# Three constant matmuls ahead of the wait for an item's sums, in a deformable convolution

## The chip, the cores and the metric

The kernel runs on one core of a Trainium2 chip. Five engines with a queue of instructions each work side by side and meet at semaphores: PE (matrix multiplications and transposes, results to PSUM), DVE and ACT (arithmetic on tiles), POOL (here it issues the gathers and does some additions), SP (plain DMAs). The metric is the device time of one execution, in microseconds (us). Lower is better.

## What is computed

The input x is f32 of shape (4, 128, 48, 48). Two stages with residual additions:

```
x = x + deformable_conv(group_norm(x))     # 3x3, then batch norm over all images, ReLU
x = x + conv3x3(group_norm(x)) + bias
```

The deformable convolution first computes 27 maps with an ordinary 3x3 convolution: for each of the nine taps a shift in y, a shift in x and a mask (a sigmoid). Each output point then reads, for each tap, four neighbouring points of the normalised image around the shifted position, weights them bilinearly, multiplies by the mask, and a 128x128 matrix per tap turns the 128 channels into outputs, summed over the taps.

## The kernel before, in words

The image points are cut into 24 chunks (ALL) of 384 points, six per image. A chunk has three tiles of 128 points and nine taps, so 27 pairs of tap and tile. Pairs are worked on in items of three: in most chunks an item is one tap over the three tiles; in the first and the last chunk (BY_TILE) an item is three taps of one tile, and the very last item is cut in two. There are 217 items in all, numbered s in the code.

One item passes through these steps:

- POOL issues one indirect DMA per pair (L377), which gathers for 128 points the four neighbours with 128 channels each from a table in HBM into g. It runs ahead of the rest: before item s it waits until the transposes of item s - 4 are done (semaphore turned, LEAD = 4).
- ACT weighs the first neighbour (L644, into a PSUM bank PA), DVE the three others (L858), and DVE adds the four up in three additions (L870, L872, L874). The last one writes acc and raises sum_step.
- PE transposes the item's three tiles (turn_item, L484) from acc into one of two PSUM banks, TP[s % 2], columns 0 to 383 of 512, and raises turned.
- ACT copies the bank to cols (copy_cols, L625) and raises copied. In most chunks ACT does so for the item two before the one that it has just weighed (copy_lag).
- PE multiplies cols by the tap's matrix into the chunk's bank CO (conv_item, L472), waiting for copied. This too runs two items behind the transposes, or one in tile-wise chunks (conv_lag).

PE's own order within an item is written out in its loop: a part of the offset convolution for a chunk two ahead (offset_conv, L432, one or two taps in most items), then the conv of an earlier item with its wait for copied, then turn_item with its wait for sum_step. At some items more follows: transposes of offsets (L441) and of masks (L447), and sums for the next image's group norm. DVE computes positions, weights and indices of the next chunk in between (indices, L797 to L833), starting from PE's transposed offsets.

The kernel already has matmuls whose results nobody reads: warm_up (L427) multiplies gavg, a constant 128x128 matrix, by itself into a bank that is free. It runs at the start, around the batch norm, and with three matmuls in items 4, 5 and 6 of the last chunk. f32 matmuls are recorded as two MATMULs and two weight loads each, f32 transposes as one of each.

After the last item come the batch norm's statistics, the ReLU, the second group norm and the second convolution, which are not touched.

Of the kernel before, what the change touches and what calls it, by code (L numbers as in the profile page):

```python
# [9 lines left out]
P = 128  # L10
# [5 lines left out]
CP = TILES * P  # L16
# [69 lines left out]
def items(c):  # L86

    if c not in BY_TILE:
        return [[(k, t) for t in range(TILES)] for k in range(TAPS)]
    return [[(k, t) for k in taps] for t in range(TILES) for taps in (LAST_SETS if (c, t) == (ALL - 1, TILES - 1) else TAP_SETS)]  # L90


def first_item(c):
    return sum(len(items(i)) for i in range(c))
# [15 lines left out]
def part_count(c):  # L110

    return c + 2
# [25 lines left out]


WARM_ITEMS = (4, 5, 6)  # L140
BANDS = 4
BR = H // BANDS
BP = BR * W
# [11 lines left out]
def build(nc, x_d, tab_d, woff_d, wconv_d, w1_d, boff_d, par_d, grid_d, out_d):  # L155

    with ExitStack() as ctx:
        def sb(name, shape, dt=F32):
            return ctx.enter_context(nc.sbuf_tensor(name, shape, dt))

        def ps(name):
            return ctx.enter_context(nc.psum_tensor(name, [P, 512], F32))

        def sem(name):
            return ctx.enter_context(nc.semaphore(name))
# [21 lines left out]
        gavg = sb("gavg", [P, P])  # L187
# [17 lines left out]
        wt0 = sb("wt0", [P, 2, TILES, 9])  # L205
        bst = sb("bst", [P, 2 * BANDS, 6])
        mv = sb("mv", [P, 2])
# [17 lines left out]
        TP = (ps("TP0"), ps("TP1"))  # L225
# [37 lines left out]
        sum_step = sem("sum_step")  # L263
# [45 lines left out]
        def add_band(eng, b, j):  # L309
            s = b * HW + j * BP  # L310
            return eng.tensor_tensor(x[:, s:s + BP], x[:, s:s + BP], o[:, s:s + BP], ALU.add)  # L311
# [10 lines left out]
        def _(sp):  # L322
# [11 lines left out]
            sp.dma_start(w1[:], w1_d).then_inc(w1_in, 16)  # L334
            for n in range(B * BANDS):
                sp.wait_ge(finished, 2 * n + 2)
                sp.dma_start(out_d[:, n * BP:(n + 1) * BP], x[:, n * BP:(n + 1) * BP]).then_inc(stored, 16)
            sp.wait_ge(stored, 16 * B * BANDS)

        @block.gpsimd  # L340
        def _(pl):
# [40 lines left out]
            def add(b):  # L382
                for j in range(0, BANDS, 2):
                    pl.wait_ge(relued, b * BANDS + (BAND_ORDER.index(j) + 1))
                    add_band(pl, b, j).then_inc(added, 1)
# [20 lines left out]
        def _(pe):  # L406
# [70 lines left out]
            def turn_item(c, i):  # L477
                units = items(c)[i]
                s = first_item(c) + i
                pe.wait_ge(sum_step, (s + 1) * 4)  # L480
                if c in BY_TILE and s > 1:
                    pe.wait_ge(copied, s - 1)
                for n in range(len(units)):
                    last = nc.tensor.transpose(TP[s % 2][:, n * P:(n + 1) * P], acc[:, s % SUMS, n, :], ident[:])  # L484
                last.then_inc(turned, 1)
# [24 lines left out]
            for c in range(ALL):  # L510
# [3 lines left out]
                for k in range(len(items(c))):  # L514
# [8 lines left out]
                    while convs <= first_item(c) + k - conv_lag(c) and (c, k) != (ALL - 1, len(items(c)) - 1):  # L523
                        conv_item(*order[convs])
                        convs += 1
                    if c == ALL - 1 and k in WARM_ITEMS:
                        pe.wait_ge(wt_ready, part_count(c))
                        warm_up(3, OMT)
                    turn_item(c, k)
                    if ahead and turn_place(c + 1) == (c, k):  # L530
                        turn_offsets(part_count(c + 1) - 1)
# [497 lines left out]
```

## Time and profile before

| | |
|---|---|
| Time of the runs | 1061.64, 1062.0 and 1064.07 us, median 1062.0 us |
| Profiled execution | span 1061.3 us from first to last instruction; no other time of it is recorded |
| PE | 763.8 us (72%), 2436 MATMULs |
| DVE, ACT | 803.4 us (76%), 378.9 us (36%) |
| POOL | 669.4 us (63%) |
| Mean granted TensorE clock | 0.780 of full speed |
| Indirect gathers | 648, 169.91 MB |

Busy times are shares of the span. The granted clock has two levels here, 0.5 (1.2 GHz) and 1.0 (2.4 GHz); a mean in between is a mixture of them. In rows of the timeline the columns are start, duration, engine, line, operation, tiles out and in, count, and in brackets the idle time of the engine before it with what ended it. "remote" stands there where the semaphore changed at a time that no recorded end of an instruction explains, "issue" where the profile shows nothing that was waited for.

### The profile page before, as it was taken

To read this page: it belongs to the slowest core of one execution; us is meant where nothing else is said; L and a number is where in the kernel's file an instruction comes from. 1 tells how busy PE (TensorE), PEld (TensorE's weight loads), DVE (VectorE), ACT (ScalarE), POOL (GpSimd) and SP (SyncE) were. 2 spreads that over 40 slices of the span, in tenths; PEclk is the share of its full clock that TensorE was granted. 3 is DMA by queue.
4 is the path that set the end of the run, shared out by engine and by line. 5 is a ranking of instruction groups with operands and counts; after the bars stand their busy time and mean duration, and the time that the engine had idled before them with its cause. 6 is when DMAs were issued, how large, how long until landed. Compare 5 with 4: busy or idle time off the path is not lost.

```text
span 1061.3 us, 8955 instructions
## 1 busy us (share of the span) xinstructions
PE 763.8 (72%) x2436; PEld 354.9 (33%) x2436; DVE 803.4 (76%) x1533; ACT 378.9 (36%) x1026; POOL 669.4 (63%) x731
## 2 busy tenths in 40 slices
PE   6787777676766867666768667674776676579998
PEld 5342222322222222222223223221222222267776
DVE  3788788787878778786878778786888787867664
ACT  2333334433333335333424334332433333343320
POOL 3666666666666666666666666666666667635661
PEclk9677677778768668977867867976878775579999
DMA  8666666666666666666566665666666666630111
GB/s 290 185 171 185 187 191 185 176 189 184 185 178 188 186 183 189 189 189 182 166 185 191 189 187 169 186 186 181 181 186 189 186 188 189 175 113 23 51 50 56
DMA packets 56245, 181.38 MB, mean 171 GB/s; under 512 B 11012, under 2 KB 12036, under 8 KB 55812
## 3 DMA queue, kind: packets, MB, share of 16 engines
q0 software_dynamic: 51840, 169.91, 55.8%
q1 hardware_dynamic: 3924, 10.32, 2.6%
q10 hardware_dynamic: 432, 0.59, 0.2%
q8 instruction: 19, 0.31, 0.1%
q14 instruction: 30, 0.25, 0.1%
HBM read 176.06 MB, written 4.72 MB: 170 GB/s over the span
## 4 chain that ended last, share of the span: by engine, by line
POOL 39%; issue 16%; DVE 16%; PE 14%; another core or an unknown queue 10%; DMA 3%; ACT 2%; DVEq 0%; POOLq 0%; ACTq 0%
POOL g L377 39%; DVE g L858 5%; DMA g<-corner_table,idx 3%; DVE PA L870 2%; DVE PA L872 2%; PE TP L564 2%; PE PA L564 2%; PE CO L564 2%; DVE acc L874 2%; PE OMT L432 2%; PE TP L484 1%; PE VU L564 1%; PE OMT L564 1%; PE CO L472 1%
## 5 line engine op out<-in xcount | busy, mean ns | idle before, releaser
L377 POOL DMA_INDIRECT g<-corner_table,idx x648 | 613.5, 947 | 327.5 <-issue 188.9
L472 PE MATMUL CO<-cols,wcs 128*128 128x384 f32 (+1 forms) x504 | 261.2, 622 | 123.2 <-issue 64.7
L644 ACT ACTIVATE PA<-g,wt 128x128 f32<-128x128 f32 x642 | 203.0, 357 | 400.2 <-DMA g<-corner_table,idx 171.5
L858 DVE TENSOR_TENSOR g<-g,PA 128x1152 f32<-128x1152 f32 (+1 forms) x217 | 291.3, 1342 | 68.6 <-DMA g<-corner_table,idx 58.9
L432 PE MATMUL OMT<-xn,woff 128*27 128x384 f32 (+2 forms) x450 | 208.4, 576 | 43.1 <-DVE wt L828 21.7
L484 PE MATMUL TP<-ident,acc 128*128 128x128 f32 x648 | 145.1, 344 | 118.5 <-DVE acc L874 60.3
L472 PEld LDWEIGHTS CO<-cols,wcs 128*128 128x128 f32 x504 | 94.1, 241 | 285.8 <-issue 186.0
L484 PEld LDWEIGHTS TP<-ident,acc 128*128 128x128 f32 x648 | 92.4, 173 | 261.0 <-DVE acc L874 114.5
L870 DVE TENSOR_TENSOR PA<-g,PA 128x384 f32<-128x384 f32 x214 | 120.3, 562 | 59.6 <-ACT PA L644 22.9
L872 DVE TENSOR_TENSOR PA<-g,PA 128x384 f32<-128x384 f32 x214 | 120.3, 562 | 18.1 <-DVE PA L870 7.6
L874 DVE TENSOR_TENSOR acc<-g,PA 128x384 f32<-128x384 f32 x214 | 118.4, 553 | 15.2 <-DVE PA L872 4.9
L625 ACT ACTIVATE cols<-TP 128x384 f32<-128x384 f32 (+1 forms) x217 | 102.0, 470 | 66.9 <-remote 46.1
L432 PEld LDWEIGHTS OMT<-xn,woff 128*27 128x27 f32 x450 | 39.2, 115 | 109.8 <-issue 78.7
L319 POOL TENSOR_TENSOR g<-xn 128x288 f32<-128x288 f32 (+1 forms) x60 | 41.5, 726 | 31.7 <-ACT xn L719 30.5
L458 PE MATMUL CO<-vt,ut 9*128 9x384 f32 (+1 forms) x56 | 35.6, 730 | 0.0
L797 DVE SCALAR_TENSOR_TENSOR low<-OMT,grid 128x54 f32<-128x54 f32 (+2 forms) x25 | 5.2, 208 | 34.5 <-remote 27.0
L607 ACT ACTIVATE mask<-OMT 128x27 f32<-128x27 f32 (+2 forms) x25 | 4.8, 192 | 62.4 <-remote 23.9
L618 ACT ACTIVATE vt<-VU 9x384 f32<-9x384 f32 x24 | 11.4, 476 | 43.2 <-remote 31.0
L427 PE MATMUL PA<-gavg 128*128 128x128 f32 x128 | 18.2, 306 | 2.9 <-POOL gavg L354 2.6
L447 PE MATMUL VU<-ident,vsum 128*9 128x128 f32 x72 | 16.0, 346 | 4.2 <-issue 4.2
L611 ACT ACTIVATE std<-OMT,eps 128x1 f32<-128x1 f32 x4 | 1.0, 262 | 50.4 <-PE OMT L413 50.4
L311 POOL TENSOR_TENSOR x<-x,o 128x576 f32<-128x576 f32 x8 | 12.1, 1524 | 10.9 <-ACT o L707 10.8
(132 smaller groups left out, 545.8 us busy)
## 6 DMA issues: line engine op xcount, KB each, us to landing
g<-corner_table,idx POOLq DMA_INDIRECT x648, 3.4
out_dram<-x SPq DMA_DIRECT2D x16, 288.0 KB, 2.1
x<-x_dram SPq DMA_DIRECT2D x3, 1152.0 KB, 7.6
x<-x_dram ACTq DMA_DIRECT2D x3, 192.0 KB, 4.0
x<-x_dram SPq DMA_DIRECT2D x3, 192.0 KB, 3.8
wconv<-wconv_dram SPq DMA_DIRECT2D x1, 576.0 KB, 5.0
w<-w_dram SPq DMA_DIRECT2D x1, 576.0 KB
grid<-grid_dram SPq DMA_DIRECT2D x1, 162.0 KB, 4.1
```

Source lines behind the costliest of these rows:

```text
L319: return eng.tensor_tensor(mixed[:, m, first:first + rows, :], p, q, op)
L377: pl.indirect_dma_start(out=g[:, k, t].rearrange("p q c -> p (q c)"), out_offset=None, in_=tab_d, in_offset=bass.IndirectOffsetOnAxis(ap=i ...
L432: last = nc.tensor.matmul(OM[:, first * W:(first + rows) * W], woff[:, k, :], xn[:, row + k // 3:row + k // 3 + rows, k % 3:k % 3 + W], st ...
L472: last = nc.tensor.matmul(co_bank(c, t)[:, t * P:t * P + size], wcs[:, c // CHUNKS % 2, k, :], cols[:, s % TURNS, n * P:n * P + size], sta ...
L484: last = nc.tensor.transpose(TP[s % 2][:, n * P:(n + 1) * P], acc[:, s % SUMS, n, :], ident[:])
L564: last = nc.tensor.matmul(MX[h % 2][m][:, 0:HB], w, mixed[:, m, r:r + BR, :], start=(ky == 0), stop=(ky == 2))
L625: nc.scalar.activation(cols[:, s % TURNS, 0:size], TP[s % 2][:, 0:size], ACT.Copy).then_inc(copied, 1)
L644: last = nc.scalar.activation(first[:, n] if s < LAST_SUMS else g[:, k, t, 0, :], g[:, k, t, 0, :], ACT.Copy, scale=wt0[:, c % 2, t, k:k + 1])
L858: nc.vector.tensor_tensor(corners[:, :, 1:4, :], corners[:, :, 1:4, :], weights[:, :, 1:4].unsqueeze(3).to_broadcast([P, size, 3, P]), ALU ...
L870: nc.vector.tensor_tensor(some, corners[:, :, 1, :], some, ALU.add).then_inc(sum_step, 1)
L872: nc.vector.tensor_tensor(some, corners[:, :, 2, :], some, ALU.add).then_inc(sum_step, 1)
L874: nc.vector.tensor_tensor(acc[:, s % SUMS, 0:size, :], corners[:, :, 3, :], some, ALU.add).then_inc(sum_step, 1)
```

## The change

PE's turn_item issues three matmuls of gavg by gavg into columns 384 to 511 of the bank that the item's transposes will fill. They stand ahead of the wait for the item's sums. The wait for copied, which tile-wise chunks have, comes before them, since it guards the bank.

```
+KEEP_WARM = 3
...
             def turn_item(c, i):
                 units = items(c)[i]
                 s = first_item(c) + i
-                pe.wait_ge(sum_step, (s + 1) * 4)
                 if c in BY_TILE and s > 1:
                     pe.wait_ge(copied, s - 1)
+                for _ in range(KEEP_WARM):
+                    nc.tensor.matmul(TP[s % 2][:, CP:CP + P], gavg[:], gavg[:], start=True, stop=True)
+                pe.wait_ge(sum_step, (s + 1) * 4)
                 for n in range(len(units)):
                     last = nc.tensor.transpose(TP[s % 2][:, n * P:(n + 1) * P], acc[:, s % SUMS, n, :], ident[:])
                 last.then_inc(turned, 1)
```

Nothing else is changed.

## Rows read from the trace of the kernel before

**Rows 1.** The page's shares of the chain that ended last, by engine.
```profile
POOL 39%; issue 16%; DVE 16%; PE 14%; another core or an unknown queue 10%; DMA 3%; ACT 2%; DVEq 0%; POOLq 0%; ACTq 0%
```

**Rows 2.** Windows: stretch, length, each engine's busy time, granted clock, DMA share, GB/s.
```profile
16.20:944.40 928.20, 641.52 (x1848) 256.17 (x1847) 724.48 (x1337) 343.82 (x971) 613.51 (x648) 0.75 0.64 185
...
589.50:593.00 3.50, 0.17 (x1) 0.00 (x0) 3.03 (x5) 0.88 (x4) 0.60 (x2) 0.79 0.52 146
593.00:598.30 5.30, 5.28 (x12) 2.08 (x12) 2.91 (x5) 1.69 (x5) 4.08 (x5) 0.50 0.52 147
598.40:608.00 9.60, 6.34 (x22) 2.37 (x21) 7.15 (x9) 3.81 (x12) 7.16 (x9) 1.00 0.73 209
885.00:919.00 34.00, 19.93 (x43) 8.76 (x43) 27.56 (x52) 11.99 (x35) 22.73 (x24) 0.50 0.63 183
```

**Rows 3.** Groups: count, busy us, mean ns, idle before and what ended it.
```profile
L377 POOL DMA_INDIRECT g<-corner_table,idx x648 | 613.5, 947 | 327.5 <-issue 188.9
...
L484 PE MATMUL TP<-ident,acc 128*128 128x128 f32 x648 | 145.1, 344 | 118.5 <-DVE acc L874 60.3
```

**Rows 4.** Timeline of POOL's gathers, three of them after a long wait.
```profile
571.32 0.94 POOL L377 DMA_INDIRECT g<-corner_table,idx  x1 [2.55 <-remote]
...
592.71 0.94 POOL L377 DMA_INDIRECT g<-corner_table,idx  x1 [2.90 <-remote]
593.96 0.94 POOL L377 DMA_INDIRECT g<-corner_table,idx  x1 [0.30 <-issue]
...
600.21 0.95 POOL L377 DMA_INDIRECT g<-corner_table,idx  x1 [0.31 <-issue]
...
738.42 0.94 POOL L377 DMA_INDIRECT g<-corner_table,idx  x1 [3.94 <-remote]
```

**Rows 5.** POOL's waits: total us, times, longest.
```profile
POOL g L377 <- remote: 99.1, 34, 3.9
...
POOL g L377 <- PE TP L484: 23.7, 12, 3.5
```

**Rows 6.** Timeline of PE around the gather at 592.71.
```profile
588.25 0.55 PE L484 MATMUL TP<-ident,acc 128*128 128x128 f32 x3 [0.94 <-DVE acc L874]
...
593.02 1.65 PE L472 MATMUL CO<-cols,wcs 128*128 128x384 f32 x2 [3.34 <-ACT cols L625]
594.46 0.85 PE L484 MATMUL TP<-ident,acc 128*128 128x128 f32 x3
```

**Rows 7.** Timeline of ACT in the same stretch.
```profile
592.47 0.49 ACT L625 ACTIVATE cols<-TP 128x384 f32<-128x384 f32 x1 [2.62 <-remote]
```

**Rows 8.** Timeline of PE over the last items.
```profile
940.84 1.49 PE L427 MATMUL OMT<-gavg 128*128 128x128 f32 x6
942.12 0.85 PE L484 MATMUL TP<-ident,acc 128*128 128x128 f32 x3
...
944.50 0.83 PE L427 MATMUL OMT<-gavg 128*128 128x128 f32 x6
945.16 0.49 PE L484 MATMUL TP<-ident,acc 128*128 128x128 f32 x3
...
948.08 0.94 PE L472 MATMUL CO<-cols,wcs 128*128 128x128 f32 x6 [0.58 <-ACT cols L625]
948.96 0.44 PE L484 MATMUL TP<-ident,acc 128*128 128x128 f32 x2
950.31 0.33 PE L484 MATMUL TP<-ident,acc 128*128 128x128 f32 x1 [0.91 <-DVE acc L868]
```

**Rows 9.** Timeline of PE and POOL at the first transposes.
```profile
31.16 0.81 PE L484 MATMUL TP<-ident,acc 128*128 128x128 f32 x3
...
33.49 0.94 POOL L377 DMA_INDIRECT g<-corner_table,idx  x1 [2.44 <-PE TP L484]
```

**Rows 10.** Timeline of DVE at the last item's sums.
```profile
949.96 0.29 DVE L868 TENSOR_TENSOR acc<-g 128x128 f32<-128x128 f32 x1
```

**Rows 11.** Timeline of ACT and DVE in the last chunk.
```profile
931.59 0.49 ACT L625 ACTIVATE cols<-TP 128x384 f32<-128x384 f32 x1 [5.71 <-remote]
...
934.56 0.56 DVE L870 TENSOR_TENSOR PA<-g,PA 128x384 f32<-128x384 f32 x1 [5.00 <-ACT PA L644]
```

More of the change, by code:

```diff
@@ L140 @@
 WARM_ITEMS = (4, 5, 6)
+KEEP_WARM = 3
 BANDS = 4
@@ L479, in turn_item @@
                 s = first_item(c) + i
-                pe.wait_ge(sum_step, (s + 1) * 4)
                 if c in BY_TILE and s > 1:
                     pe.wait_ge(copied, s - 1)
+                for _ in range(KEEP_WARM):
+                    nc.tensor.matmul(TP[s % 2][:, CP:CP + P], gavg[:], gavg[:], start=True, stop=True)
+                pe.wait_ge(sum_step, (s + 1) * 4)
                 for n in range(len(units)):
```

## The prediction

> **What bounds it now.** I read the page first. The chain that ended last is POOL's for 39%, and 10% stands under "another core or an unknown queue" [rows 1]. PE is no bound by that view: it is busy 641.5 us of the 928.2 us from the first gather to the last [rows 2], a stretch I call the gather stage. Next the groups by line: POOL issues 648 gathers of 947 ns [rows 3], one each 1.25 us, because 0.30 or 0.31 us of issue time follows each [rows 4]. That makes 648 x 1.25 = 810 us, so 118 us of the stage go elsewhere. POOL's waits name them: 34 waits on "remote" with 99.1 us and 12 on PE's transposes with 23.7 us [rows 5].
>
> The timeline shows what such a wait is. PE's transposes that start at 588.25 are over at 588.80, and every earlier item's too [rows 6]. ACT's copy of a turned item still starts only at 592.47, after 2.62 us on "remote" [rows 7], and POOL's next gather at 592.71 [rows 4]. So both see PE's count of turned items late, some 2.6 us after POOL has stopped issuing. The length of these waits is regular. After 12 gathers without one it is 2.55 us, after 15 2.90, after 21 3.94 [rows 4], the gathers between counted in the same view. Each gather issued adds (3.94 - 2.55) / 9 = 0.15 us to the next wait, whatever PE, ACT and DVE did in between. 648 x 0.15 = 97 us, most of the 118. I read this as a debt that POOL's pace runs up and pays at the next stop: an earlier or later stop changes when it is paid, hardly how much. Why the count is seen late no row shows.
>
> **What the change adds.** Each of the 217 items gets three f32 matmuls of 128x128 on gavg, recorded as two MATMULs each, so 1302 MATMULs and as many weight loads. They wait for nothing new: the wait on copied, which stands in tile-wise chunks alone, only moves ahead of the wait on sums and was met before the conv in front of it. They signal nobody. No DMA is added, and nothing on ACT, DVE or POOL.
>
> Their price stands in the trace, because the last chunk already runs three such matmuls ahead of three of its items. At half clock the six MATMULs start at 940.84 and the transposes behind them at 942.12: 1.28 us. At full clock, 944.50 to 945.16: 0.66 us [rows 8]. Over 217 items that is 143 to 278 us of PE time; at the stage's mean granted clock of 0.75 [rows 2], half of the time at each level, 210 us.
>
> What covers it: PE idles 118.5 us in front of its transposes, waiting for sums [rows 3]. That is exactly where the new matmuls stand, so at most 118 us lie beside DVE's work. The rest, 92 us or 0.4 us an item, with 1.28 at most in any one, pushes transposes later. PE's idle time in front of a conv is no cover: it stands there before it reaches the new matmuls.
>
> What a later transpose costs: the gather of an item asks for the transposes of four items before. Those at 594.46 to 595.31 [rows 6] are what the gather at 600.21 needs, and it waits for nothing beyond its 0.31 us [rows 4]: 4.9 us of slack in an item just after a late count, where PE is furthest behind. If PE comes out of such a stop at half clock, as here, it does one or two items with 1.28 us more each, 2.6 us, and keeps 2.3 us. Where the slack is gone, POOL stops a little earlier and, by the debt above, waits less at the next stop. I take 0 for the gather stage. Bounds: below, 10 us off, from the chain view of the stage (the first rival); above, 15 us on (the second). Between them stand the 12 waits on transposes, 23.7 us in all, the only ones where PE's own lateness is on record.
>
> What the matmuls may give: a fuller PE and a higher clock. From 885 to 919 PE has 19.93 us of work in 34 and the granted clock is 0.50 throughout [rows 2]; with 1.28 us more for each of some eight items it is busy some 30 of 34. Three transposes take 0.85 us at half clock and 0.49 at full [rows 8]. That makes PE quicker between its waits, but PE is not what its neighbours wait for; I count it as paying for the 92 us, no more.
>
> A rule speaks against the gain, and the trace bears it out first: from 589.5 to 593 PE does 0.17 us of work, and from 593 to 598.3 it has 0.50, in full use [rows 2]. The Trainium skill (TensorE: Matmul & The Clock Gate, section "Why this matters for your kernels") says that idle gaps between bursts of matmuls bring the lower clock back. The stops that make these gaps stand before a conv, with the added matmuls behind it, so by the rule the clock falls there as before and the sum stays at no gain.
>
> The head: the first transposes start at 31.16, and POOL's fifth item waits for them until 33.49 [rows 9]. PE has no idle time there, so they come 1.28 us later at half clock; POOL loses between 0 (if the count would have been seen late anyway) and 1.3 us. I take 0.6.
>
> The tail: DVE hands over the last sums at 949.96 + 0.29 = 950.25 [rows 10] and the last transpose follows at 950.31 [rows 8], so PE is on time by 0.06 us. The items turned at 945.16 and 948.96, with one between, follow each other through transposes, ACT's copy and a conv, 1.9 us a round, and each round gets 0.66 us more; PE shows no idle time in front of 948.96 that would hide it. Three rounds of 0.66 and the 0.66 of the last item itself, less the idle 0.91 us in front of 950.31 [rows 8], make +1.7. Against it, a higher clock ahead of 943 brings PE into these rounds earlier: by 0.36 us for the transposes and 0.7 for the conv (1.65 at half clock [rows 6], 0.94 at full [rows 8]), so 1.1 us if one item is affected and 2.2 if two have piled up. I take the first, +0.6, with ends at -0.5 and +1.7.
>
> Sum: 1061.3 (the span) + 0 + 0.6 + 0.6 = 1062.5 us. The median of the runs is 1062.0, 0.7 above the span, so on their scale 1063.2.
>
> One thing spreads this without a sign. In the last chunk one late count holds ACT for 5.71 us and through it DVE for 5.00 [rows 11]. Where the stops fall shifts with every microsecond, and a chunk of 38 us has one or two of them. I allow 4 us either way.
>
> **Rivals.** First, faster: the clock stays full and the pieces of the chain where PE itself is late at half clock shrink. For it: the 0.50 of a 34 us stretch, and 12 POOL waits with PE as releaser. The Trainium skill (same page, section "Part 4: PE-mode transpose") says that transposes don't raise the clock as matmuls do; these added ones are matmuls. Against it: the debt, which would be paid anyway. Price: half of the 23.7 us off and the 1.2 of head and tail on, -10.6: 1051 us. Chance 0.17.
>
> Second, slower: PE oversubscribed at half clock. An item then needs one offset tap, a conv (1.65), transposes (0.85) [rows 6, 8] and 1.28 more; with the tap taken as long as the conv, 5.4 us, over the stage's 928.2 / 217 = 4.28. If the clock doesn't rise while PE catches up, three or four items in a row fall behind by 1.1 us each and eat the 4.9 us of slack. From there on POOL stops on transposes. It decides where the slack is under 2 us; if the 12 waits on transposes become twice as many with the same 2 us, less what later stops give back, it is about +15: 1078 us. Against it: from 598.4 on the clock is at full after such a stop already now [rows 2]. Chance 0.15.
>
> Third, slower by more: the delay with which PE's count is seen grows with the number of PE's instructions, which rises by 0.7 in the stage (1302 on 1848 MATMULs [rows 2]). For it: only PE's signals are late. Against it: the length of the waits follows the gathers alone. Price, if the 99.1 us grow by half as much as the instructions, 0.35: +35, 1097 us. Chance 0.06.
>
> That the matmuls don't lift the clock at all, so that the change doesn't do what it is for, leaves the forecast where it is; it is inside its 0.62.
>
> **Numbers.** The forecast holds 0.62, with 1058 to 1069 as its own range. With 4 us of scatter around +1.2 it gives same (within 0.3%, 3.2 us, which is what a measurement of this kernel can tell) 0.40, slower 0.15, faster 0.07. With the rivals: faster 0.24, same 0.40, slower 0.36. The range of 1053 to 1080 leaves out half of the first rival, the third and the far part of the second, some 0.18.
>
> **What would show it.** Right: POOL's "remote" waits again near 99 us in 30 to 40 pieces, 0.15 us per gather, PE busier by about 200 us and its idle time before the transposes nearly gone, the mean clock of the stage above 0.75 and the time unchanged. The first rival shows as POOL waits on PE's transposes well under 23.7 us and a gather stage shorter by ten; the second as those waits doubled; the third as "remote" waits that are longer for the same number of gathers. I am wrong at the root if the waits on "remote" change their slope, because then PE does take part in the debt.

## The result and the profile after

The changed kernel takes 1075.4 us, the kernel before 1063.0 us beside it on the same chip (medians of four runs each). The ratio is 1.0114, 95% interval 1.0094 to 1.0133: 12.4 us slower. The range of 1053 to 1080 holds that, but the likeliest case does not, whose own range ended at 1069. The profiled execution of after took 1077.5 us with a span of 1075.7, 14.4 above the span of before.

PE first, where the added work is. From the page of after the line of PE, then the chain by engine.

```profile
PE 826.4 (77%) x3738; PEld 523.6 (49%) x3738; DVE 805.7 (75%) x1533; ACT 378.5 (35%) x1026; POOL 670.3 (62%) x731
...
POOL 29%; PE 28%; issue 16%; another core or an unknown queue 10%; DVE 10%; DMA 4%; ACT 3%; SPq 0%; DVEq 0%; ACTq 0%; POOLq 0%
```

The groups by line of after (count, busy us, mean ns, idle before), and its gather stage as a window (the columns of [rows 2]):

```profile
L378 POOL DMA_INDIRECT g<-corner_table,idx x648 | 614.4, 948 | 337.9 <-issue 177.6 <-remote 111.0 <-PE TP L487 34.5
L484 PE MATMUL TP<-gavg 128*128 128x128 f32 x1302 | 210.4, 305 | 2.6 <-issue 2.6
L487 PE MATMUL TP<-ident,acc 128*128 128x128 f32 x648 | 124.9, 307 | 23.4 <-issue 11.3 <-DVE acc L877 8.6 <-DVE PA L875 2.5
```

```profile
16.00:955.60 939.60, 700.37 (x3123) 420.84 (x3122) 727.27 (x1337) 343.38 (x971) 614.35 (x648) 0.87 0.63 184
```

The added matmuls are busy on PE for 210.4 us. The 210 of the prediction counted something else, from the start of the added matmuls to the start of the transposes; summed that way over the trace of after, idle time left out, it is 187 us. PE's idle time before the transposes fell from 118.5 us [rows 3] to 23.4, the granted clock of the stage rose from 0.75 [rows 2] to 0.87, and the transposes went from 344 to 307 ns. Yet PE's share of the chain doubled from 14% [rows 1], and the stage grew from 928.2 us to 939.6. That is +11.4 of the 14.4; the other 3 lie after the last gather (9.5 us to the last transposes there, 6.3 before).

POOL's gathers cost the same. What grew is the idle time in front of them, 327.5 us [rows 3] to 337.9, and POOL's waits in after (total us, times, longest) say in which way:

```profile
POOL g L378 <- remote: 111.0, 47, 3.1
POOL g L378 <- PE TP L487: 34.5, 18, 3.2
```

There were 34 and 12 of them before [rows 5], so 46 became 65: more waits, not longer ones. The timeline of POOL in after shows the new pattern; the lines left out between two of these are 11 gathers with 0.30 or 0.31 us in front.

```profile
827.67 0.94 POOL L378 DMA_INDIRECT g<-corner_table,idx  x1 [2.58 <-remote]
...
844.95 0.95 POOL L378 DMA_INDIRECT g<-corner_table,idx  x1 [2.55 <-remote]
...
862.21 0.95 POOL L378 DMA_INDIRECT g<-corner_table,idx  x1 [2.54 <-PE TP L487]
```

The same stretch before; 17 gathers without a stop are left out between the first two lines, 14 between each of the next:

```profile
807.88 0.94 POOL L377 DMA_INDIRECT g<-corner_table,idx  x1 [3.00 <-remote]
...
833.55 0.94 POOL L377 DMA_INDIRECT g<-corner_table,idx  x1 [3.46 <-remote]
...
854.92 0.94 POOL L377 DMA_INDIRECT g<-corner_table,idx  x1 [2.91 <-remote]
...
876.36 0.94 POOL L377 DMA_INDIRECT g<-corner_table,idx  x1 [2.97 <-remote]
```

A stop after 12 gathers waits 2.55 us in after, just as before [rows 4]. The medians over all stops (defined below) say the same: 2.56, 2.98 and 3.44 us after 12, 15 and 18 gathers before; 2.09, 2.58 and 2.97 us after 9, 12 and 15 in after. The slope is untouched. But starts lie 17.28 us apart over 12 gathers and 25.67 over 18, so a gather costs 8.39 / 6 = 1.398 us, and 17.28 - 12 x 1.398 = 0.50 us is left over that is paid by the stop. I call a gap of over 0.7 us in front of a gather a stop. Counted so, the profile of before has 46 and that of after 62: 16 more at 0.50 are 8 of the 10.4 us of added idle time. The remaining 2.4 I can't put in one place. The line does not hold for the shortest distances: stops after only three gathers, four in each profile, wait 1.6 to 2.9 us, where it gives 1.2.

### The profile page after: what moved, and what is told of

The parts are those of the page before. It is cut to its first block, busy times and chain, and to the rows that moved or that the text cites. A ratio compares the mean times of both kernels' runs of the same rounds, so it can differ in the third digit from the quotient of the medians.

```text
span 1075.7 us, 11542 instructions
## 1 busy us (share of the span) xinstructions
PE 826.4 (77%) x3738; PEld 523.6 (49%) x3738; DVE 805.7 (75%) x1533; ACT 378.5 (35%) x1026; POOL 670.3 (62%) x731
## 4 chain that ended last, share of the span: by engine, by line
POOL 29%; PE 28%; issue 16%; another core or an unknown queue 10%; DVE 10%; DMA 4%; ACT 3%; SPq 0%; DVEq 0%; ACTq 0%; POOLq 0%
POOL g L378 29%; PE CO L473 5%; PE TP L484 4%; PE OMT L433 4%; DMA g<-corner_table,idx 4%; PE TP L487 3%; DVE g L861 3%; PE TP L567 2%; PE PA L567 2%; PE CO L567 2%; DVE PA L873 1%; DVE PA L875 1%; ACT PA L647 1%; DVE acc L877 1%
## 5 line engine op out<-in xcount | busy, mean ns | idle before, releaser
L378 POOL DMA_INDIRECT g<-corner_table,idx x648 | 614.4, 948 | 337.9 <-issue 177.6
L473 PE MATMUL CO<-cols,wcs 128*128 128x384 f32 (+1 forms) x504 | 227.7, 550 | 164.2 <-issue 102.1
L484 PEld LDWEIGHTS TP<-gavg 128*128 128x128 f32 x1302 | 209.0, 221 | 69.3 <-issue 28.3
L473 PEld LDWEIGHTS CO<-cols,wcs 128*128 128x128 f32 x504 | 82.9, 214 | 297.9 <-issue 209.9
L433 PE MATMUL OMT<-xn,woff 128*27 128x384 f32 (+2 forms) x450 | 181.4, 510 | 47.6 <-DVE wt L831 25.4
L484 PE MATMUL TP<-gavg 128*128 128x128 f32 x1302 | 210.4, 305 | 2.6 <-issue 2.6
L487 PE MATMUL TP<-ident,acc 128*128 128x128 f32 x648 | 124.9, 307 | 23.4 <-issue 11.3
L487 PEld LDWEIGHTS TP<-ident,acc 128*128 128x128 f32 x648 | 86.4, 159 | 37.4 <-issue 21.1
L433 PEld LDWEIGHTS OMT<-xn,woff 128*27 128x27 f32 x450 | 36.5, 107 | 103.0 <-issue 72.5
L459 PE MATMUL CO<-vt,ut 9*128 9x384 f32 (+1 forms) x56 | 25.3, 535 | 0.0
```

What stands on the lines that cost most here:

```text
L378: pl.indirect_dma_start(out=g[:, k, t].rearrange("p q c -> p (q c)"), out_offset=None, in_=tab_d, in_offset=bass.IndirectOffsetOnAxis(ap=i ...
L433: last = nc.tensor.matmul(OM[:, first * W:(first + rows) * W], woff[:, k, :], xn[:, row + k // 3:row + k // 3 + rows, k % 3:k % 3 + W], st ...
L473: last = nc.tensor.matmul(co_bank(c, t)[:, t * P:t * P + size], wcs[:, c // CHUNKS % 2, k, :], cols[:, s % TURNS, n * P:n * P + size], sta ...
L484: nc.tensor.matmul(TP[s % 2][:, CP:CP + P], gavg[:], gavg[:], start=True, stop=True)
```

## Why are there more stops? Theories

Both POOL's gather at 844.95 and ACT's copy below wait for the transposes of item 187, which end at 837.18 + 0.55 = 837.73 in after:

```profile
837.18 0.55 PE L487 MATMUL TP<-ident,acc 128*128 128x128 f32 x3
...
840.91 0.55 PE L487 MATMUL TP<-ident,acc 128*128 128x128 f32 x3 [0.27 <-DVE acc L877]
...
845.26 0.91 PE L473 MATMUL CO<-cols,wcs 128*128 128x384 f32 x2 [3.04 <-issue]
846.01 1.30 PE L484 MATMUL TP<-gavg 128*128 128x128 f32 x6
847.10 0.85 PE L487 MATMUL TP<-ident,acc 128*128 128x128 f32 x3
```

```profile
844.71 0.49 ACT L628 ACTIVATE cols<-TP 128x384 f32<-128x384 f32 x1 [2.28 <-remote]
```

So PE's release (the raising of the semaphore that others wait for) comes 7.0 us late at two receivers at the same moment, in the last quarter microsecond of POOL's stop, as in [rows 4, 6, 7]. PE itself is not held up meanwhile: it goes on to the next item and has turned that too by 841.46, so late instructions for PE don't explain it. Of the 24 copies by ACT in the trace of before that start over 1 us after their transposes, with ACT idle for over 0.5 us in front, 21 start inside a stop of POOL; in after 36 of 38. POOL waits for the same release, so this alone doesn't show which of the two ends the other. That the length of a stop follows the gathers before it, and e5 below, speak for POOL's stop letting the release through.

- **Theory A:** after a stop PE's releases arrive at once until a certain number of PE instructions has started. Later ones are held until POOL stops again. More PE instructions per item bring the stops closer together, and each has a fixed price.
- **Rival B:** PE's added time makes its own transposes late.
- **Rival C:** fuller columns or the higher clock disturb the others.

## Experiments

All ratios are against the kernel before, run beside each kernel on the same chip, with 95% intervals. The kernel before took 1063 to 1072 us on these chips, so the microseconds in the expectations are to be read against its 1062.

**The same count with one column, and a third of the count with the same columns.**

```
-  matmul(TP[s % 2][:, CP:CP + P], gavg[:], gavg[:], ...)          # three times
+  matmul(TP[s % 2][:, CP:CP + 1], gavg[:], gavg[:, 0:1], ...)     # e1: three times
+  matmul(TP[s % 2][:, 0:CP], gavg[:], wconv[:, 0:3, :], ...)      # e2: once
```

> As the changed kernel, but each of the three added matmuls moves 1 column in place of 128: the same number of PE instructions, little PE time. Theory A (a release by PE reaches POOL late once some number of PE instructions has followed it, so POOL stops more often, about 66 times in place of 44, and each stop has a fixed price of about 0.45 us): slower than before by 8 to 14 us, about 1072 to 1077, POOL's waits on remote events near 111 us as in the changed kernel. Rival B (the added PE time makes the transposes and convolutions late): as before, 1060 to 1065, remote waits near 99 us. Rival C (the higher granted clock, or what PE's busier columns do to the rest): as before as well, as nearly no columns are added.

> As the changed kernel, but one matmul of 384 columns an item in place of three of 128: the same columns and PE time added, a third of the PE instructions. Theory A (count of PE instructions): a third of the changed kernel's loss, 1065 to 1068, some 50 stops of POOL. Rivals B and C (PE time, clock): as the changed kernel, 1073 to 1078.

Measured: e1 1.0168 (1.0142 to 1.0195), e2 1.0038 (1.0019 to 1.0057). The groups of the added matmuls, e1 and then e2:

```profile
L484 PE MATMUL TP<-gavg 128*128 128x1 f32 x1302 | 204.0, 272 | 0.0
```

```profile
L484 PE MATMUL TP<-wconv,gavg 128*128 128x384 f32 x434 | 210.8, 573 | 0.0
```

e2 adds the same PE time as the change, 210.8 against 210.4 us, and costs a third of its loss: rival B falls. (Counted from start to start, as in the prediction, it is 187 us in both.) e1 adds nearly no columns, its granted clock over the run stays at 0.771 (before 0.780, after 0.889), and it loses more, not nothing: rival C falls. e1's expectation was wrong on one thing, since a one-column matmul still takes 272 ns: its PE time isn't little, so e1 alone does not speak against B. Theory A's 1.003 to 1.006 for e2 is hit; for e1 it gave up to 14 us, 1.013, too little.

The count itself can be read from windows that start where a release got through, 0.25 us before POOL's gather, and end at the end of two successive transposes, the last that arrived in time and the first that was held. The numbers in brackets are PE's matmuls and weight loads. Before, then after, e1 and e2:

```profile
786.20:796.39 10.19, 9.65 (x27) 4.04 (x28) 7.57 (x12) 3.75 (x11) 7.57 (x8) 0.67 0.59 166
786.20:800.16 13.96, 11.87 (x33) 4.71 (x33) 10.57 (x15) 5.05 (x14) 10.40 (x11) 0.76 0.64 178
```

```profile
827.40:834.10 6.70, 6.12 (x26) 3.84 (x27) 3.21 (x5) 2.39 (x7) 4.91 (x6) 0.75 0.51 152
827.40:837.72 10.32, 9.74 (x43) 5.68 (x44) 6.60 (x10) 4.00 (x12) 7.61 (x9) 0.83 0.57 166
```

```profile
855.85:862.96 7.11, 6.55 (x23) 5.01 (x24) 3.62 (x5) 2.78 (x8) 5.34 (x6) 0.50 0.50 152
855.85:868.24 12.39, 11.84 (x39) 8.28 (x40) 8.49 (x25) 5.10 (x15) 9.40 (x10) 0.50 0.62 176
```

```profile
827.75:838.13 10.38, 8.29 (x31) 3.90 (x32) 6.66 (x10) 4.13 (x12) 7.69 (x9) 1.00 0.58 171
827.75:841.75 14.00, 11.74 (x42) 5.24 (x43) 9.50 (x13) 5.30 (x15) 10.44 (x11) 1.00 0.61 179
```

In these windows the last good release comes 6.7 to 10.4 us after the stop, the first held one 10.3 to 14.0. In instructions that is 47 to 63 and 66 to 87. The table has the medians over every stop that comes at least three items after the one before it. "Held" are the transposes that the stopped gather asks for, "in time" those of one item earlier; times and counts run to their ends. The last column is PE's busy time up to the held ones.

| kernel | stops counted | in time: us, PE instructions | held: us, PE instructions | PE busy, us |
|---|---|---|---|---|
| before | 39 | 11.0, 55 | 15.5, 71 | 12.1 |
| after | 54 | 6.5, 51 | 10.3, 78 | 8.4 |
| e1, one column | 56 | 6.0, 48.5 | 10.3, 77.5 | 8.8 |
| e2, one wide matmul | 46 | 9.8, 52 | 13.9, 73 | 11.4 |
| e11, fewer taps (below) | 35 | 14.5, 53 | 18.5, 66 | 14.0 |

From kernel to kernel the times change by a factor of 2.4 (in time) and 1.8 (held), PE's busy time by 1.7, the counts by less than 1.2. The middle between the two counts is 60 to 65 in all five. That is theory A's footprint. It holds for medians: for single stops the middle half of the held counts runs from 66 to 75 before and from 72 to 90 in after. The number of stops goes with it: 46 before, 52 in e2, 62 in after, 66 in e1. The losses over the added stops are 0.7 us a stop in e2, 0.8 in after and 0.9 in e1, more than the 0.50 of the line, so a part of a stop's price stays unexplained.

**POOL one item further ahead.** `LEAD = 4` becomes 5 in the changed kernel (e3) and in the kernel before (e4); the five buffers of sums allow it.

> The changed kernel with POOL allowed to run 5 items ahead of the transposes in place of 4. Theory A: the stops come up to 5 items apart in place of 4, some 52 in place of 66, so about 0.45 us x 14 = 6 us faster than the changed kernel, 1067 to 1070. Rivals B and C: POOL's lead hides lateness of 1 us more, or changes nothing: 1073 to 1078 by C, between 1064 and 1070 by B.

> The kernel before with POOL allowed to run 5 items ahead in place of 4. Theory A: the stops, 5 to 6 items apart now, come 6 to 7 items apart, some 36 in place of 44, so 3 to 4 us faster than before: 1058 to 1060. If the lead doesn't set the stops (the wait on remote events is a debt by the gather, whenever it is paid): no change, 1061 to 1064.

Measured: 1.0179 (1.0153 to 1.0204) and 1.0097 (1.0074 to 1.0120), both slower than with a lead of 4. My arithmetic that the lead spaces the stops was wrong: e4 has 56 stops against 46, 12 of them after three gathers, and e3 has 70. The median distance stays at 15 gathers in e4 and falls from 12 to 9 in e3, so a longer lead spaces nothing. Theory A foresaw both the wrong way; why the short stops appear is open.

**POOL off PE's releases.** POOL waits for DVE's sums, and DVE waits for the transposes that free a buffer of sums.

```
-  pl.wait_ge(turned, first_item(c) + i - LEAD + 1)
+  pl.wait_ge(sum_step, (first_item(c) + i - LEAD + 1) * 4)
   ...
+  if s >= SUMS:
+      dve.wait_ge(turned, s - SUMS + 1)          # ahead of the write to acc
```

> The kernel before, but POOL waits for the sums of the item four back (a release by DVE) in place of its transposes (a release by PE), and DVE itself waits for the transposes before it reuses a buffer of sums. Theory A as the first four runs leave it (a release by PE is seen late once some 60 to 75 PE instructions have started since POOL last stopped): no release by PE reaches POOL any more, so the stops are now set by DVE's instructions, far fewer an item; if DVE's releases come late by the same count, stops 8 items apart or more, at most 25 of them, 8 to 10 us faster than before, ratio 0.991 to 0.993. If lateness has nothing to do with the sender: stops as before, ratio 0.998 to 1.002.

> The changed kernel with the same edit: POOL waits for DVE's sums, not for PE's transposes. Theory A (the loss is the lateness of PE's releases at POOL): the added matmuls no longer cost, within 0.3% of the run beside it that has this edit without the matmuls, and below it if the higher clock is worth something. Rival B (PE's time makes the transposes late): still 6 to 12 us above that run, since acc buffers and cols wait for PE as before.

> As the run of the kernel before with POOL waiting for DVE's sums, and POOL let run 8 items ahead. If the distance of the stops follows the lead: half as many stops as with a lead of 4, some 5 us faster than that run. If, as with the lead of 5 above, the distance doesn't follow the lead, or POOL's transfers then wait elsewhere: no gain, ratio to it 1.00 to 1.02.

Measured: e5 (without the matmuls) 1.0847 (1.0812 to 1.0881), e6 (with them) 1.1409 (1.1360 to 1.1459), e7 (lead 8) 1.1236 (1.1204 to 1.1268). All my expectations missed: I had taken the lateness for something between PE and POOL. ACT's waits of e5 and of e6 show that PE's releases to others are late too:

```profile
ACT cols L625 <- remote: 221.2, 32, 12.3
```

```profile
ACT vt L621 <- remote: 157.8, 22, 10.5
ACT mask L610 <- remote: 110.8, 19, 8.4
ACT cols L628 <- remote: 92.4, 15, 13.1
```

Before, the first of these was 46.1 us in 19 waits. In e5, item 160 is turned at 784.00 (first line below), and ACT copies it at 800.40, 16.4 us later:

```profile
783.45 0.55 PE L484 MATMUL TP<-ident,acc 128*128 128x128 f32 x3
```

```profile
800.40 0.49 ACT L625 ACTIVATE cols<-TP 128x384 f32<-128x384 f32 x1 [12.29 <-remote]
```

POOL's gathers around it:

```profile
795.92 0.95 POOL L377 DMA_INDIRECT g<-corner_table,idx  x1 [0.30 <-issue]
803.85 0.94 POOL L377 DMA_INDIRECT g<-corner_table,idx  x1 [6.99 <-DVE acc L878]
```

The release arrives 3.5 us after POOL's last gather is over (796.87), in a stop that POOL spends waiting for DVE and not for this release. That is the best evidence that a pause lets it through. A pause is not the only way, though: of 34 such copies in e5, 22 start inside a stop of POOL, and 12 start 5.9 to 13.9 us late while POOL goes on issuing, as this one, whose transposes end at 70.67, with POOL issuing without a pause from 61.94 to 84.14:

```profile
79.66 0.49 ACT L625 ACTIVATE cols<-TP 128x384 f32<-128x384 f32 x1 [5.36 <-remote]
```

POOL now stops when DVE has run dry, so a held release is let through later, and the stops get longer: 55 of them with 220.5 us in all in e5, 46 with 131.3 us before. I read from this that POOL's wait on PE in each item is worth its price; no run separates it from the wait on transposes that the same edit gives to DVE. Here the three matmuls cost 1.1409 / 1.0847 = 1.052, some 58 us, with 58 stops of 264.1 us in e6.

**Spreading POOL's pauses.** One addition on unused elements on POOL after each item's gathers: 128 columns (e8), 192 (e9), and 192 in the changed kernel (e10).

```
+  pl.wait_ge(paced, first_item(c) + i)
+  pl.tensor_tensor(idle[:], gavg[:], gavg[:], ALU.add).then_inc(paced, 1)
```

> The kernel before with an addition on 128x128 unused elements on POOL after each item's gathers, some 0.4 us an item, which no one waits for. If the wait at a stop is a debt of 0.15 us by the gather that has to be paid somewhere (0.45 us an item) plus 0.45 us a stop: the added time is taken out of the waits, which fall from about 99 us on remote events to under 40, and the total stays within 6 us, ratio 0.995 to 1.005. If the waits are for the late release and not for a debt: all 216 x 0.4 = 86 us are added, ratio 1.06 to 1.09.

> The kernel before with 192 columns of unused addition on POOL an item in place of the 128 of the run above: that one lengthened an item by 0.28 us (starts of its gathers 4.05 us apart by the item), this one should by about 0.45 us, which is 3 gathers x 0.15 us, the whole debt. Theory D (PE's releases are held back for every receiver while POOL's gathers leave a backlog, and let through when POOL pauses): with no backlog nothing is held, the stops mostly go, and the waits of 114 us shrink to under 20 for 97 us added: ratio 0.985 to 0.998. If a stop is needed after so many PE instructions whatever the backlog: some 26 stops of about 0.9 us beside the added 97 us, ratio 1.003 to 1.010.

> The changed kernel with the same 192 columns on POOL an item. Theory D (no backlog, nothing held): the added matmuls cost nothing here, ratio to before as that of the run without them within 0.003, or below it by what the higher clock is worth. If a stop is needed after so many PE instructions whatever the backlog: half as many stops again, 12 x 0.9 = 10 us above that run. Rival B (PE's time): 6 to 12 us above that run.

Measured: e8 1.0033 (1.0018 to 1.0047), e9 1.0049 (1.0031 to 1.0066), e10 1.0123 (1.0104 to 1.0141). The additions of e8 and POOL's waits there:

```profile
L384 POOL TENSOR_TENSOR idle<-gavg 128x128 f32<-128x128 f32 x217 | 90.2, 416 | 4.0
```

```profile
POOL g L379 <- remote: 48.0, 25, 2.6
```

90 us of work on the engine that the chain runs through cost 3.5 us: they came out of the waits (remote 99.1 to 48.0, where under 40 was expected, on transposes 23.7 to 9.9). So the 0.15 us by the gather is a debt that any pause of POOL pays, as predicted. But the stops do not vanish with the debt. In e9, where an item's gathers start 4.17 us apart instead of 3.76 and so little debt is left, a stop still has the same form:

```profile
530.22 0.52 POOL L384 TENSOR_TENSOR idle<-gavg 128x192 f32<-128x192 f32 x1
532.48 0.96 POOL L379 DMA_INDIRECT g<-corner_table,idx  x1 [1.74 <-remote]
```

e9 has 27 stops and e10 44, by the idle time in front of a gather, and the matmuls still cost 0.0074 between them, 8 us. Theory D is out: it gave e9 0.985 to 0.998. In both expectations the line "whatever the backlog" holds. Held releases now need more PE instructions (median 117 in e8, 141 in e9, 114 in e10, counted as in the table), so the count is no constant: small pauses raise it. None of these versions beats the kernel before.

**Fewer PE instructions, and the last chunk.** e11 is the kernel before without taps 1 to 7 of the offset convolution; e12 is the changed kernel without the matmuls in the last chunk.

```
   for k in taps:
+      if c and 0 < k < TAPS - 1:
+          continue                                             # e11
-  for _ in range(KEEP_WARM):
+  for _ in range(KEEP_WARM if c < ALL - 1 else 0):             # e12
```

> The kernel before, with 7 of the 9 taps of the offset convolution left out in every chunk but the first (the offsets that come out are other ones; every gather still moves as much): some 320 matmuls and as many weight loads fewer, 13% of PE's instructions. Theory A (PE's releases are held after a number of PE instructions since POOL last stopped): the stops lie 13% further apart, 40 in place of 46, each saving 0.45 to 1.1 us: 3 to 7 us faster than before, ratio 0.993 to 0.997. If the number of PE instructions doesn't matter in this direction: ratio 0.998 to 1.002.

> The changed kernel with the three matmuls left out in the last chunk alone, where items are short and the end of the gathers is followed by a chain on PE. If the last chunk's tail costs what the two profiles differ by between the last gather and the last transposes (9.5 against 6.3 us): 3 us faster than the changed kernel, ratio to before 1.008 or 1.009. If it costs 0.6 us as predicted: 1.010 to 1.012.

Measured: e11 0.9975 (0.9957 to 0.9993), slightly faster. That lies between the two forecasts (0.993 to 0.997, 0.998 to 1.002), and the interval reaches into both. The median distance of its stops grew from 15 gathers to 18, but several short ones kept their number at 47, so the gain isn't explained by a count of stops. It also takes PE time away, and so fits rival B; only the count of the table above tells them apart here. e12: 1.0096 (1.0077 to 1.0116), which overlaps the 1.0114 of the change; whether the last chunk costs 0.6 or 3 us is not settled. In its profile the last transposes follow the last gather by 6.3 us, as before.

## Why the prediction was wrong in its middle

- **PE's price** (143 to 278 us, taken 210) lay in its bounds; that the busy time came to 210.4 us is luck. Counted as the prediction counted it, it is 187 us, because the clock of the stage rose to 0.87; by the two prices that clock gives 0.74 x 143 + 0.26 x 278 = 178. The cover was right (idle time before the transposes fell by 95 of at most 118.5 us), and so was the direction of the clock. "PE busier by about 200 us" was not: the busy time of the stage rose by 59 us, from 641.5 [rows 2] to 700.4, partly since the transposes, the convs (622 to 550 ns) and the offset convs (576 to 510 ns) became shorter.
- **The gather stage, taken as 0, was the step that failed**, +11.4 us. "An earlier or later stop changes when it is paid, hardly how much" is right for the part by the gather (e8 shows it) and wrong for the whole wait. I fitted a slope through 2.55, 2.90 and 3.94 us and did not look at what is left at zero gathers: 2.55 - 12 x 0.15 - 0.30 = 0.45 us was in [rows 4] all the time. With it, the number of stops has a price, and I had nothing that set their number: there were 62 stops in place of 46.
- **The third rival was the right mechanism in the wrong form**, at a chance of 0.06. PE's instructions do delay PE's releases (e1, e2, e6), but they show as stops closer together, not as longer waits. The evidence that I held against it, that the length of a wait follows the gathers alone, holds for the medians from twelve gathers on and says nothing on how often a wait comes. So the test that I named, a changed slope, could not have found it.
- **The second rival** named about the right time for a wrong reason. POOL's waits on transposes rose from 12 to 18, but e2 has 33 of them (41.6 us) with a third of the loss. Whether such a wait is put down to "remote" or to PE says little: the stop that ends at 862.21 in after stands under PE, yet the transposes that it asks for ended at 855.82. The range reached to 1080 because of this rival alone, so that it held 1075.4 is luck.
- **The first rival's gain is real and too small.** e1 and the change add the same instructions; what the change has more is columns and clock, and it loses 0.0054 less (the intervals don't touch), some 6 us. I read this as the added instructions costing some 18 us and the clock returning 6: +12.
- **The rule on the clock** held at the stops, though the stage's mean rose. In after PE does 0.72 us of work from 841.5 to 845.2; the transposes before take 0.55 us and the ones at 847.10 take 0.85. The Trainium skill (TensorE: Matmul & The Clock Gate, section "Why this matters for your kernels") says that idle gaps bring the lower clock back, and the trace agrees; windows of after:

```profile
841.50:845.20 3.70, 0.72 (x2) 0.02 (x1) 3.12 (x5) 1.42 (x5) 1.15 (x2) 1.00 0.60 176
845.20:846.40 1.20, 1.14 (x5) 0.88 (x6) 1.20 (x1) 1.20 (x6) 0.90 (x2) 0.92 0.00 0
846.40:850.00 3.60, 3.60 (x17) 2.99 (x16) 1.74 (x4) 0.53 (x2) 2.69 (x4) 0.55 0.70 203
```

- **The scale.** I added 0.7 us to get from the span to the time of a run; where both are on record they differ by 1.8 us.
- **The head**, +0.6, was 0. The first transposes came earlier, at 29.66 against 31.16 [rows 9], and POOL's fifth item starts at 33.39 in after against 33.49 [rows 9], since its release was late anyway:

```profile
29.66 0.55 PE L487 MATMUL TP<-ident,acc 128*128 128x128 f32 x3 [1.39 <-issue]
```

- **The tail**, +0.6 (-0.5 to +1.7), was +3.2 in the profile; a part is plain, since the last item's transposes now stand behind six added MATMULs though its sums are there (963.73 + 0.29 = 964.02):

```profile
964.17 0.83 PE L484 MATMUL TP<-gavg 128*128 128x128 f32 x6
964.84 0.27 PE L487 MATMUL TP<-ident,acc 128*128 128x128 f32 x1
```

```profile
963.73 0.29 DVE L871 TENSOR_TENSOR acc<-g 128x128 f32<-128x128 f32 x1
```

That is 0.82 us between sums and transpose, where it was 0.06. The rest I have not taken apart. PE came out of a late wait at half clock shortly before:

```profile
949.57 1.65 PE L473 MATMUL CO<-cols,wcs 128*128 128x128 f32 x6 [5.11 <-ACT cols L628]
```

e1 and e2, which add matmuls in the last chunk too, have 7.5 and 7.6 us from the last gather to the last transposes in place of 9.5, so +3.2 is not the plain price of the matmuls there.

## What to carry to other kernels

When waits follow a line, read its intercept as well as its slope, and ask what sets how many there are. Instructions put into an engine's idle time are not free by that alone: beside a stream of gathers on POOL, PE's instruction count had a price of its own, 1302 matmuls of one column cost 1.7%, 434 of 384 columns 0.4%. Where such filler is wanted, issue few and wide; here even that was slower than none.

## What the runs showed of the hardware

Under a stream of indirect gathers from POOL, PE's releases were held for ACT, DVE and POOL alike, up to 7.9 us before and 16.4 us in e5, and came through mostly when POOL paused (36 of 38 late copies in after, 22 of 34 in e5). By medians, those that arrived in time came within about 50 PE instructions after a pause, the held ones at 66 to 78, over spans from 6 to 18 us. Not settled: what holds them, what lets some through without a pause, whether matmuls and weight loads count alike (they came in equal numbers here), why small pauses raise the count to 114 to 141, and why a longer lead of POOL made both kernels slower. A 128x1 f32 matmul with its own weights took 272 ns at a granted clock of 0.77, hardly less than the 305 ns of 128 columns at 0.89.
